# Second mixture of experts: the last expert's outputs in three PSUM banks, and GpSimd waiting for landings among its indirect transfers

## What is computed

```python
N, cap = B * S, int(1.25 * B * S / E)              # 2048 tokens, 320 rows per expert
probs = softmax(x @ gate_w.T)
top2_w, top2_idx = top_k(probs, 2)
a_e, a_w, tok_id = top2_idx.reshape(-1), top2_w.reshape(-1), arange(2 * N) // 2
valid = (bincount(a_e, length=E) <= cap)[a_e]
p = where(valid, minimum(pos, cap - 1), cap)       # pos: rank of the pick within its expert
buf = zeros((E, cap + 1, H)).at[a_e, p].set(x[tok_id])
h = silu(einsum('ech,efh->ecf', buf, w1) + b1[:, None, :])
y = einsum('ecf,egf->ecg', h, w2) + b2[:, None, :]
out = (y[a_e, p] * (a_w * valid)[:, None]).reshape(N, 2, H).sum(axis=1)
x = layernorm(x + out)
```

## Time and profile before

| | |
|---|---|
| median of three runs | 1129.98 us |
| the profiled execution's own time | 1137.67 us |
| its span, first to last instruction | 1135.9 us |
| mean granted TensorE clock | 0.972 of full |
| TensorE busy | 1007.0 us (89%), 8628 matmuls |
| VectorE busy | 617.5 us (54%) |
| ScalarE busy | 425.0 us (37%) |
| GpSimd busy | 255.6 us (22%), 282 instructions |
| DMA: HBM read, written | 46.13 MB, 33.03 MB |

### The profile page before, as it was taken

The page is one execution under the profiler, slowest core; times in us unless marked ns, Lnnn a source line. Parts: engine busy times, 40 slices in busy tenths (PEclk is TensorE's granted clock), DMA queues, the critical chain, the costliest instruction groups (busy, mean ns, idle before and its releaser), DMA issues.

```text
span 1135.9 us, 20834 instructions
## 1 busy us (share of the span) xinstructions
PE 1007.0 (89%) x8628; PEld 717.5 (63%) x8628; DVE 617.5 (54%) x1398; ACT 425.0 (37%) x557; POOL 255.6 (22%) x282
## 2 busy tenths in 40 slices
PE   6989989989988899999998798989879987986887
PEld 3666566666675798996445474656656574753656
DVE  2653753652767573333335836656574669655333
ACT  1523533524524356555431434152415423340212
POOL 0310310220120333333331120231103112103642
PEclk9999999999987899999999899999999999997999
DMA  6013412211400891111112000200110010005527
GB/s 188 1 43 112 147 43 97 98 43 65 131 1 1 326 323 44 50 48 48 38 48 84 1 6 1 85 2 5 41 34 2 6 38 1 2 1 154 153 89 235
DMA packets 64237, 80.50 MB, mean 71 GB/s; under 512 B 12736, under 2 KB 57680, under 8 KB 63120
## 3 DMA queue, kind: packets, MB, share of 16 engines
q1 hardware_dynamic: 53392, 61.15, 16.3%
q0 software_dynamic: 5664, 15.47, 4.2%
q10 hardware_dynamic: 5088, 2.56, 0.9%
HBM read 46.13 MB, written 33.03 MB: 70 GB/s over the span
## 4 chain that ended last, share of the span: by engine, by line
PE 46%; issue 21%; DVE 16%; ACT 12%; DMA 2%; POOL 2%; SPq 1%; another core or an unknown queue 1%; ACTq 0%; DVEq 0%; POOLq 0%
PE ps L1517 8%; DVE sb_arena L871 6%; ACT sb_arena L642 6%; PE ps L1653 5%; PE ps L1675 4%; PE ps L1778 3%; PE ps L1723 3%; DVE sb_arena L875 3%; PE ps L1561 2%; PE ps L1990 2%; PE ps L1625 2%; DVE ps L892 2%; PE ps L1852 1%; PE ps L1696 1%; PE ps L2005 1%
## 5 line engine op out<-in xcount | busy, mean ns | idle before, releaser
L642 ACT ACTIVATE sb_arena<-ps 77x2048 f32<-77x2048 f32 (+1 forms) x64 | 116.5, 1883 | 27.8 <-PE ps L1607 26.6
L1383 POOL TENSOR_TENSOR sb_arena<-sb_arena,sb_neghalf 128x2 f32<-128x2 f32 x40 | 28.7, 719 | 398.4 <-DVE sb_arena L837 398.4
L1517 PE MATMUL ps<-sb_arena,sb_wreg 128*128 128x256 f32 (+1 forms) x512 | 108.5, 360 | 6.8 <-issue 3.8
L1517 PEld LDWEIGHTS ps<-sb_arena,sb_wreg 128*128 128x128 f32 (+1 forms) x512 | 87.6, 192 | 23.2 <-issue 8.3
L1852 PE MATMUL ps<-sb_arena 128*128 128x128 f32 x800 | 99.3, 278 | 3.3 <-DVE sb_arena L1246 2.3
L1625 PE MATMUL ps<-sb_arena 32*77 32x256 f32 (+1 forms) x1024 | 77.6, 420 | 27.0 <-ACT sb_arena L642 14.5
L1852 PEld LDWEIGHTS ps<-sb_arena 128*128 128x128 f32 x800 | 96.0, 194 | 5.4 <-issue 3.1
L754 ACT ACTIVATE sb_arena<-sb_arena 128x1024 f32 x72 | 76.0, 1057 | 16.9 <-issue 12.3
L1625 PEld LDWEIGHTS ps<-sb_arena 32*77 32x77 f32 (+1 forms) x1024 | 43.7, 175 | 47.5 <-ACT sb_arena L642 25.6
L871 DVE TENSOR_REDUCE sb_arena<-ps 128x8 f32<-128x2048 f32 x32 | 71.0, 2282 | 3.5 <-PE ps L1581 3.5
L1561 PE MATMUL ps<-sb_headrow,sb_identb 128*32 128x512 bf16 (+1 forms) x266 | 64.7, 380 | 1.4 <-DVE sb_arena L875 1.3
(11 more groups left out here) (285 smaller groups left out, 1891.1 us busy)
## 6 DMA issues: line engine op xcount, KB each, us to landing
sb_arena<-in_m_w SPq DMA_DIRECT2D x8, 1536.0 KB, 9.5
sent<-sb_xres SPq DMA_DIRECT2D x32, 256.0 KB
sb_arena<-outs SPq DMA_DIRECT2D x16, 512.0 KB, 5.8
outs<-sb_zeros SPq DMA_DIRECT2D x4, 1664.0 KB, 9.7
sent<-sb_zeros SPq DMA_DIRECT2D x2, 2560.0 KB, 13.7
sb_arena<-in_m_w SPq DMA_DIRECT2D x16, 256.0 KB
early<-sb_xres SPq DMA_DIRECT2D x12, 256.0 KB, 2.9
sb_arena<-in_xT SPq DMA_DIRECT2D x8, 256.0 KB, 3.5
```

What stands on the lines that cost most here:

```text
L642: nc.scalar.activation(dst, src, ACT.Exp).then_inc(S(f"h_PT{p}"), 1)
L1517: ins = mm(dst[:, m * cols:(m + 1) * cols], wt[0:rows, k, m * P:(m + 1) * P], src[0:rows, k, 0:cols], start=(k == 0), stop=(k == KC - 1))
```

## The change

The last expert's three output parts are written to three PSUM banks, 6, 7 and 2 (`LAST_BANKS`). For this expert TensorE signals `e_y` once per part, and VectorE waits once per part. TensorE adds the residual rows of sequences 0, 1 and 3 early, and those of 2 and 4 to 7 behind the last adds. `IDLE_MIXED` goes from 24 to 8.

GpSimd's loop over experts is written out: ten gathers for experts 0 to 3; scatter of 0; gathers of 4 and 5 (each behind a wait for the landing of the gathers of 0 and 1); a wait for the landing of gather 5; scatter of 1; a wait for gather 2; gather 6; waits for the landing of gathers 6 and 3; gather 7; scatters of 2 and 3; a wait for the landing of all scatters of experts 0 to 3; scatters of 4 to 7.

```diff
@@ -54,9 +54,10 @@
 HOTS = 2 * EARLY
 LATE_CHOOSE, LATE_RANK, LATE_HOTS, LATE_TABLE, LATE_QUANTA, LATE_RAW, LATE_INDEX, LATE_WEIGHTS = 0, 2, 3, 5, 6, 8, 9, 10
 FAR = 128 * P
+LAST_BANKS = (6, 7, 2)
 HIDDEN = 3
 IDLE, IDLE_SPLIT, IDLE_CLIP = 96, 4, (4, 6)
-IDLE_TURN, IDLE_LAYERS, IDLE_ROWS, IDLE_SCORES, IDLE_RESULT, IDLE_MIXED, IDLE_ROUTE = 4, 50, 20, 4, 12, 24, 2
+IDLE_TURN, IDLE_LAYERS, IDLE_ROWS, IDLE_SCORES, IDLE_RESULT, IDLE_MIXED, IDLE_ROUTE = 4, 50, 20, 4, 12, 8, 2
 FILL = (PICKS + E * CAP) // 4
 CODE = (127 + 7) * P
 CLAMP = 10000.0
@@ -481,6 +482,8 @@
         def y1_at(e, tile, rows):
 
             nth = tile - parts_of(e)[0][0]
+            if e + 1 == E:
+                return ps[rows, LAST_BANKS[nth], 0:D]
             return ps[rows, 4 + 2 * (e % 2) + nth // 2, D * (nth % 2):D * (nth % 2 + 1)]
 
         def mixed_of(b, t):
@@ -1322,8 +1325,10 @@
 
             def outputs1(e):
                 dve.wait_ge(S("e_y"), e + 1)
-                for tile, row, n, _ in parts_of(e):
+                for i, (tile, row, n, _) in enumerate(parts_of(e)):
                     r = slice(row, row + n)
+                    if e + 1 == E and i:
+                        dve.wait_ge(S("e_y"), E + i)
                     ins = v.tensor_tensor(y1t[r, tile, :], y1_at(e, tile, r),
                                           experts1[e % XBUFS].b2[r, :], ALU.add)
                     if e + 1 == E:
@@ -1480,15 +1485,36 @@
 
             pool.wait_ge(S("indexed"), 3)
             pool.wait_ge(S("sent1"), 16 * 2 * B)
-            for e in range(XBUFS):
-                gather1(e)
-            for e in range(E):
+            def scatter1(e):
                 for i, j in enumerate(tiles_of(e, False)):
                     pool.wait_ge(S("e_ys"), e + 1 + (i if e + 1 == E else 0))
                     g.indirect_dma_start(outs1[:, :], bass.IndirectOffsetOnAxis(ap=idx1[:, j:j + 1], axis=0), y1t[:, j, :], None
                                          ).then_inc(S("e_out"), 16)
-                if e + XBUFS < E:
-                    gather1(e + XBUFS)
+
+            def gathered(e):
+                pool.wait_ge(S(f"t_in{e % XBUFS}"), rows_at(e))
+
+            def scattered(e):
+                pool.wait_ge(S("e_out"), 16 * sum(len(tiles_of(x, False)) for x in range(e + 1)))
+
+            for e in range(XBUFS):
+                gather1(e)
+            scatter1(0)
+            for e in (4, 5):
+                gathered(e - XBUFS)
+                gather1(e)
+            gathered(5)
+            scatter1(1)
+            gathered(2)
+            gather1(6)
+            gathered(6)
+            gathered(3)
+            gather1(7)
+            scatter1(2)
+            scatter1(3)
+            scattered(3)
+            for e in range(4, E):
+                scatter1(e)
             for b in range(B):
                 ln = lnrow[:, b]
                 pool.wait_ge(S("vars"), b + 1)
@@ -1989,7 +2015,10 @@
                     for m in range(KC):
                         ins = mm(y1_at(e, tile, slice(row, row + n)), hid1[e % 2][:, m, at:at + n], b.w2[:, m, :],
                                  start=(m == 0), stop=(m == KC - 1))
-                ins.then_inc(S("e_y"), 1)
+                    if e + 1 == E:
+                        ins.then_inc(S("e_y"), 1)
+                if e + 1 < E:
+                    ins.then_inc(S("e_y"), 1)
 
             def residual1(b):
 
@@ -2006,11 +2035,13 @@
                 ins.then_inc(S("mixed"), 1)
 
             pe.wait_ge(S("store"), 2 * B)
-            for b in range(4):
+            early = [b for b in range(4) if b not in LAST_BANKS]
+            for b in early:
                 residual1(b)
             pe.wait_ge(S("e_ys"), E - 1 + len(parts_of(E - 1)))
-            for b in range(4, B):
-                residual1(b)
+            for b in range(B):
+                if b not in early:
+                    residual1(b)
             for _ in range(IDLE_MIXED):
                 mm(mixed_of(0, 0)[IDLE:P, :], zeros[:, :].bitcast(BF16)[:, IDLE:P], headrow[:, :, :].rearrange("p g k -> p (g k)")[:, 0:D], start=False,
                    stop=False, skip_group_check=True)
```

## The result

The changed kernel takes 1136.16 us in the median of 20 runs, the kernel before 1131.49 beside it: a ratio of 1.0033, interval 1.0019 to 1.0047, or 3.7 us more (so the means, 1135.12 and 1131.41; the medians lie 4.7 us apart). That is outside the range of 1119.5 to 1130.5, within the half per cent called "the same", and on the side of the slower rival. The profiled execution tells the opposite: a span of 1129.3 us against 1135.9. Both are true, and the experiments show why. Each of the two traces lies at an edge of its timed runs: the traced execution of before took 1137.67 us, above all of its twenty timed runs (1127.24 to 1136.54), that of the changed kernel 1131.05 us, near the lowest of its own (1130.35 to 1138.31).

A forecast was written before the change was run, and what follows sets the result against it. TensorE was taken to set the pace, with two stalls costing 6.4 us in the second mixture. Gaining 7.95 us took the profiled 1137.67 us to 1129.7; the median, 7.7 lower, was forecast at 1122.0, range 1119.5 to 1130.5.

The forecast's parts named there:

- the slower rival: Rival D: in the second mixture, GpSimd's pauses too short, handovers of experts 3 to 6 late; 7.6 us slower, chance 0.09.
- What bounds the kernel now: Second mixture: two stalls cost 6.4 us; a shared queue fills after eight or more unpaused indirect transfers, clear once landed.
- rival B: Second mixture: waits remove nothing in timed runs; stalls the profiler's own (first form, 1.55 us gained) or other (1.65); chance 0.32.
- the 7.95 us: Whole forecast gain at the end of the span: last scatter starts at 1100.9 instead of 1108.85.
- Last expert in parts: Last expert's outputs: adding part by part lets the third scatter go at 1107.2 instead of 1108.85, 1.65 us gained.
- The waits: GpSimd's new order: three real landing waits add 2.1, 1.5 and 1.1 us, 4.7 in all; last scatter starts at 1100.9.
- What that takes away: Second mixture: both stalls go, TensorE and last adds come 6.4 us earlier; GpSimd binds next, 7.95 us gained in all.
- Fewer fillers and the start of the mixture: Before the mixture: 16 fewer fillers save 1.86 us of TensorE, no gain of its own; gap 0.2 us, costed at nothing.
- The rival named the Trainium skill's sentence: Mixture start: if data came late it would start at 1.2 GHz, gain 6.4 instead of 7.95 us; chance 0.05.
- Code loading: Second mixture: stalls would be instruction fetches, waits worth nothing, 1128.4 us; 3 in 100, within B's chance.
- C: Second mixture: GpSimd takes over, landings take 4 us or one stall stays; gain 4.3 or 3.4 us, chance 0.13.
- D: Second mixture: queue cleared only by a real pause, so every handover of experts 3 to 6 late; 1137.6 us, chance 0.09.

The follow-up runs named there:

- e1: Kernel before with the last expert's outputs part by part in three banks alone (24 fillers, GpSimd's old order, no landing waits): ratio 0.9990.
- e15: Kernel before with the last expert's outputs part by part alone, timed again in another series: ratio 0.9991 to the kernel before.
- e14: Kernel before with nothing changed, traced again beside the repeated parts-alone kernel: ratio 1.0004.
- e5: The changed kernel as it is (8 fillers), timed again beside the kernel before: ratio 0.9983, 1136.35 us.
- e2: Kernel before with GpSimd's new order and landing waits alone (24 fillers, two banks): ratio 0.9977, 2.6 us faster.
- series 5: Runs of the later-waits kernel (1.0032) and the changed kernel (0.9950) beside the kernel before, which took 1139.3 us.
- series 2: Runs of the changed kernel with 8 and 24 fillers, the unchanged kernel and the order without waits, beside the kernel before at 1138.4 us.
- e8: Kernel before with GpSimd's new order but without the three landing waits that hold it up: ratio 1.0072, 8 us slower.
- e17: Changed kernel with 16 fillers and GpSimd's landing waits one group of transfers later: ratio 1.0032 to the kernel before.
- e3: Kernel before with 8 fillers in place of 24, nothing else: ratio 0.9993.
- e7: Kernel before with nothing changed (one empty line): ratio 1.0010.
- e18: The changed kernel once more, beside a kernel before at 1139.3 us: ratio 0.9950.
- series 3 and 4: Two sets of runs of changed and unchanged kernels in which the kernel before took 1131.7 and 1131.2 us.

## Why the prediction was wrong

**What bounds the kernel now.** The reading of the one trace was right: stalls at two spots, tied to GpSimd's run of transfers, 6.4 us. That a queue shared with the handovers fills, as I supposed, no run shows. What failed is the step to the median: I took stalls of one execution as part of every run. The hint was on the table and I gave it to rival B alone: the profiled execution took 1137.67 us, above all three runs of before (1127.99 to 1132.28). In series with a median of 1131 the trace of before has none of them: its stage is 85.6 and 86.1 us there, against 92.7 in the trace that I read, so the 7.95 us were for the most part not there to be gained. That the series of the result was a stall-free one is inferred from its 1131.49, as it was not traced.

**Last expert in parts.** 1.65 us forecast for the last scatter; 1.7 measured in e1, and 1.65 in the stall-free pair of e15 and e14 (57.44 against 59.09 us from the first gather). With 24 fillers 0.4 us of it come through in e1, so the prediction was right that this term needs fewer of them. In the changed kernel GpSimd's backlog swallows it: the last scatter starts at 60.7 us both with the parts (e5) and without them (e2). Right in size, and worth nothing there.

**The waits.** The term that was mis-sized. A landing was taken at 2.4 to 4.1 us behind its issue, with 4.7 us in all; the three took 4.72, 4.09 and 2.87 (1063.40 to 1068.12, 1074.60 to 1078.69, 1086.40 to 1089.27), from the issue to GpSimd's next one. Less 1.29 us of issue each that is 7.8 us, 7.9 by the idle times above. My upper bound of 3 x 2.8 = 8.4 held it; I chose the last two by the quiet row at the end of the span and the first by judgment, though the first two both fall beside weight loads that SP issues (at 1061.57, 1067.23 and 1073.32 us). So the last scatter starts at 60.7 us behind the first gather instead of 57.7.

**What that takes away.** Right in kind where there are stalls: no remote waits in the four traces of the changed kernel there, with either number of fillers. In size it is 0.9950 in series 5 and 0.9983 in series 2, against a forecast of 0.993. "The two meet: GpSimd is the next to bind" understated it: in the changed kernel's trace the last scatter starts 1100.78 - 1095.56 = 5.2 us behind the last output matmul, in e1 1.56, so GpSimd binds by 3.7 us. And "is clear once they have landed" was too much for the late handovers themselves: in e8 and e17 VectorE took expert 2's outputs in the midst of a run.

**Fewer fillers and the start of the mixture.** "A gap of 0.2 us" became 3.73, mostly since the data came 3 us later than in the sum; and "I cost the gap at nothing" rested on the gap of 1.96 us, which no longer was the nearest row. It cost 1.7 us in three traces of four of the changed kernel. With 24 fillers gaps of 1.59 to 1.94 us left 14.05 us in three traces; e3 did so too with 8 fillers and 1.84 us, and e2 did not with 24 fillers and 2.05 us. Nor was the row that I took a safe one: ahead of expert 3's outputs a gap of 2.09 us in e7 had 4.64 us behind it, one of 2.14 us in e3 had 3.01. The rival named the Trainium skill's sentence (TensorE: Matmul & The Clock Gate, What's actually happening) that activity releases the throttle: three of the four traces agree with its direction, 15.74 us behind 3.73 to 3.90 us with hardly any work, and e18 does not show it. In timed runs the 24 fillers did not show: 0.9974 against 0.9983, and 1.0026 against 1.0017.

**The rivals.** B was right in its first form: where the timed runs have no stalls, the waits remove nothing. Its price was wrong in sign, by the same two terms: instead of 1.55 us gained, 2.0 us later by GpSimd and, in the traces, 1.7 us of clock. Code loading is not seen beside the stalls: from 1066 to 1092 us the traces of before, e7, e8 and e17 hold no instruction packet, and that of the changed kernel holds two and no stall. C's GpSimd takes over in each trace: the sign named for it, a backlog, is there from 1089.27 on, and the 3.5 us gained in the stage are near its 4.3 and 3.4. D's late handovers happened, in e8 and e17, but not in the change, whose pauses are long enough. The last paragraph of the prediction said that a trace that is all right with a median that gains under 3 us would mean the profiler's own stalls; that was wrong too, since the same profiler shows none of them in six traces of series 3 and 4 in which GpSimd runs as densely.

**No version beat both.** The changed kernel gains where before is stalled (0.9950 and 0.9983) and costs 0.17 to 0.33% where it is not. The parts alone, or the waits one group later, lie at 0.9985 to 0.9991 in stall-free series, with intervals that reach 1.000 or more, and the latter is 0.32% slower than before in a stalled one.

## What to carry to other kernels

A stall that stands in one trace must be shown to be in the timed runs before its removal is booked as a gain: compare the traced execution's own time with the spread of the runs, and trace the unchanged kernel again in another series. A wait for a landing cost here the whole way from issue to landing less one issue period, at the DMA load of that moment (2.87 us in all behind scatters, 4.09 and 4.72 beside weight loads), and it made the issuing engine the next bound, which had less slack than that. Whoever takes fillers out on the ground that the data will come sooner should first see in a trace that they do; here the traces put 1.7 us on it, and the timed runs could not tell.

## What the runs showed of the hardware that was not expected

With the same program, handovers from TensorE to VectorE and ScalarE came late in the traces of some series (2 to 5 us in the kernel before, up to 12 us in e8) and in none of others. Where they did, the first late handover of a run was due within 0.4 us behind the start of GpSimd's ninth indirect transfer in a row, in the six cases first looked at (two in the first trace, two in e7, one each in e8 and e17), whether earlier ones had landed or not; e1 and e3 add one each (due at 1072.5 and 1065.8 us). Six of the eight lie at the same place of the schedule, so they are less than eight witnesses. And nine in a row is no condition: in e3 a handover due at 1076.6 us came 1.7 us late, five transfers behind a pause of 1.6 us. My "bad wait begins at the eighth" named the time at which VectorE ran out of work, which the schedule fixes; the time at which the handover was due is the better mark. TensorE's own work went on meanwhile, until it needed what was late. In stall-free series 22 transfers in a row did nothing of the kind. What differs between the series was not found; chips 1 and 2 each had both kinds.
